# A hypergraph block on one core: H B Hᵀ made in two halves around v and y, and a last group finished graph by graph

## The reference, cut to what matters

```python
def hypergraph_conv(x, adj, W, b):
    H = (adj != 0).astype(x.dtype)
    w = adj.reshape(N, -1)[:, :C]                 # first row of adj
    Dn = 1 / einsum('nce,ne->nc', H, w)           # 0 where the sum is not positive
    Be = 1 / H.sum(axis=1)
    xw = einsum('ncd,hd->nch', x, W)
    m = Be[:, :, None] * einsum('nce,nch->neh', H, xw)
    return Dn[:, :, None] * einsum('nce,neh->nch', H, m) + b

h = layer_norm(relu(hypergraph_conv(x, adj, W1, b1)), gamma, beta)
y = hypergraph_conv(h, adj, W2, b2) + x
out = layernorm(x + y)                            # over the last axis, no gain
```

## Time and profile before

| | |
|---|---|
| median of 3 runs | 287.64 us (287.48 to 287.89) |
| the profiled execution, its own time | 287.23 us |
| its span in the trace | 285.4 us |
| PE busy | 276.9 us (97%) |
| PEld busy | 247.8 us (87%) |
| DVE busy | 229.5 us (80%) |
| ACT busy | 196.2 us (69%) |
| POOL busy | 134.9 us (47%) |
| granted TensorE clock, mean | 0.995 |

### The profile page before, as it was taken

The page is one execution under the profiler, slowest core; times in us unless marked ns, Lnnn a source line. Parts: engine busy times, 40 slices in busy tenths (PEclk is TensorE's granted clock), DMA queues, the critical chain, the costliest instruction groups (busy, mean ns, idle before and its releaser), DMA issues.

```text
span 285.4 us, 5786 instructions
## 1 busy us (share of the span) xinstructions
PE 276.9 (97%) x1820; PEld 247.8 (87%) x1820; DVE 229.5 (80%) x646; ACT 196.2 (69%) x560; POOL 134.9 (47%) x194
## 2 busy tenths in 40 slices
PE   7999999999999999999999999999999999999991
PEld 6889899898988989898998989899898989889890
DVE  3795688887889878887978878797987879696784
ACT  3588967877767678766767776676678775573714
POOL 2341546436372744536363553636364364526362
PEclk9999999999999999999999999999999999999998
DMA  6912042344324134433433333522423332020014
GB/s 217 332 52 69 3 129 39 92 126 116 114 63 158 57 97 128 111 113 92 147 54 119 112 92 112 111 94 55 149 39 92 94 93 76 37 73 3 21 54 147
DMA packets 37270, 27.70 MB, mean 97 GB/s; under 512 B 10028, under 2 KB 35320, under 8 KB 37240
## 3 DMA queue, kind: packets, MB, share of 16 engines
q1 hardware_dynamic: 37136, 27.30, 33.8%
q10 hardware_dynamic: 104, 0.04, 0.1%
HBM read 17.21 MB, written 8.42 MB: 90 GB/s over the span
## 4 chain that ended last, share of the span: by engine, by line
PE 91%; ACT 3%; DVE 3%; issue 1%; POOL 1%; DVEq 0%; POOLq 0%; ACTq 0%
PE bank_v L303 30%; PE bank_g L320 10%; PE bank_v L337 10%; PE bank_g L313 10%; PE bank_g L315 10%; PE bank_v L281 8%; PE bank_s L262 4%; PE bank_g L330 3%; PE bank_s L402 1%; ACT ht_sb L497 1%; ACT sq_sb L555 1%; PE bank_g L383 1%; DVE bn_sb L933 1%; DVE q_sb L742 0%; DVE pair_sb L735 0%
## 5 line engine op out<-in xcount | busy, mean ns | idle before, releaser
L981 POOL TENSOR_TENSOR xb_sb<-x_sb,b_half 128x512 f32<-128x512 f32 (+1 forms) x31 | 41.1, 1329 | 76.0 <-DVE r_lo L730 51.1
L548 ACT ACTIVATE r_sb<-bank_v,vec 128x512 f32<-128x512 f32 x64 | 44.2, 690 | 38.0 <-PE bank_v L303 37.4
L313 PE MATMUL bank_g<-w_hi,r_hi 128*128 128x258 f32 x256 | 65.6, 288 | 0.0
L315 PE MATMUL bank_g<-w_lo,r_hi 128*128 128x256 f32 x256 | 63.8, 282 | 0.0
L989 POOL TENSOR_SCALAR r_hi<-r_sb 128x512 fp32r<-128x512 f32 x64 | 43.6, 682 | 39.8 <-ACT r_sb L548 39.8
L303 PE MATMUL bank_v<-u_hi,w_lo 128*128 128x512 f32 x128 | 50.8, 397 | 0.0
L303 PE MATMUL bank_v<-u_lo,w_hi 128*128 128x512 f32 x128 | 50.8, 397 | 0.0
L303 PE MATMUL bank_v<-u_hi,w_hi 128*128 128x512 f32 x128 | 50.7, 396 | 0.0
L313 PEld LDWEIGHTS bank_g<-w_hi,r_hi 128*128 128x128 f32 x256 | 48.3, 189 | 1.7 <-DVE w_lo L798 0.3
L730 DVE TENSOR_TENSOR r_lo<-r_sb,r_hi 128x512 fp32r<-128x512 f32 x64 | 48.9, 785 | 0.9 <-POOL r_hi L989 0.9
L315 PEld LDWEIGHTS bank_g<-w_lo,r_hi 128*128 128x128 f32 x256 | 48.1, 188 | 1.2
(11 more groups left out here) (119 smaller groups left out, 457.6 us busy)
## 6 DMA issues: line engine op xcount, KB each, us to landing
x_sb<-in_x_dram SPq DMA_DIRECT2D x16, 512.0 KB, 3.9
out_dram<-z_sb SPq DMA_DIRECT2D x15, 512.0 KB, 3.2
adj_sb<-in_adj_dram SPq DMA_DIRECT2D x15, 256.0 KB, 3.7
d_row<-d_rows SPq DMA_DIRECT2D x13, 256.0 KB, 3.7
w_raw<-in_L_gnn_W_dram SPq DMA_DIRECT2D x2, 512.0 KB, 4.9
out_dram<-z_sb SPq DMA_DIRECT2D x2, 256.0 KB, 2.4
adj_sb<-in_adj_dram SPq DMA_DIRECT2D x2, 128.0 KB, 2.4
turned_h<-h_sb SPq DMA_TRANSPOSE x13, 2.4
```

What stands on the lines that cost most here:

```text
L313: pe.matmul(bank_g[:, n, 0:W2COLS], r_hi[:, i % 2, k, graph(n)], w2_hi[:, k], start=(k == 0), stop=False)
L315: pe.matmul(bank_g[:, n, 0:DOUT], r_hi[:, i % 2, k, graph(n)], w2_lo[:, k], start=False, stop=False, skip_group_check=True)
L548: nc.scalar.activation(r_sb[:, k], bank_v[:, k % 2], ACT.Relu, bias=vec[:, k:k + 1]).then_inc(relu_ready, 1)
L981: nc.gpsimd.tensor_tensor(xb_sb[:, i % 2, part], x_sb[:, i % 3, part], b2_half[:, :].unsqueeze(1).to_broadcast([P, n, DOUT]), ALU.add).the ...
```

## The change

- `make_s` takes a half. For iterations 1 to 12 half 0 of s(i+3) (graphs 0 and 1) is issued between v(i+1, 3) and y(i, 0), and half 1 stays behind y(i, 1).
- At the end DVE takes the statistics of group 14 for both halves before the last group's var1, and `make_var2` of group 14 before the last `read_g`.
- The last group's graphs 2 and 3 get their own steps: `make_last_var1(n)`, one POOL power of one column each, `read_last_g(n)`, one semaphore increment for each y matmul. PE issues the identity matmuls of graphs 2 and 3 behind y of graphs 0 and 1.
- Of the last group, graphs 0 and 1 are normalised by ACT and stored by SP as before; graph 2 is normalised by ACT, with a shift that POOL makes, and stored by a DMA from ACT's queue; graph 3 is normalised by DVE and stored by SP.
- Group 14 is stored as two halves of 256 KB instead of one of 512 KB.

```diff
@@ store (SP) @@
-                if i >= 1:
+                if 1 <= i < LAST:
+                    sp.wait_ge(out_ready, i)
                     store(i - 1)
-            for half in range(2):
-                store(LAST, half)
+            sp.wait_ge(half_out_ready, 1)
+            store(LAST - 1, graphs(0))
+            sp.wait_ge(out_ready, LAST)
+            store(LAST - 1, graphs(1))
+            sp.wait_ge(last_out_ready[0], 1)
+            store(LAST, graphs(0))
+            sp.wait_ge(last_out_ready[2], 1)
+            store(LAST, slice(3, 4))
@@ PE @@
-            def make_s(j):
-                pe.wait_ge(htb_ready, j + 1)
-                pe.wait_ge(wcol_ready, j + 1)
-                if j:
+            def make_s(j, half=None):
+                if half != 1:
+                    pe.wait_ge(htb_ready, j + 1)
+                    pe.wait_ge(wcol_ready, j + 1)
                     pe.wait_ge(a_ready, min(j, ON_PE))
                     pe.wait_ge(at_ready, j)
-                for n in range(PER):
+                for n in each(half):
                     mm = pe.matmul(s_parts[:, n // 2, n % 2], ht_sb[:, j % 2, n], htb_sb[:, j % 2, n],
                                    start=True, stop=True)
-                mm.then_inc(s_made, 1)
+                if half != 0:
+                    mm.then_inc(s_made, 1)
...
+                if i and i + 3 < G:
+                    make_s(i + 3, 0)
                 make_y(i, 0)
                 make_y(i, 1)
                 if i + 3 < G:
-                    make_s(i + 3)
+                    make_s(i + 3, 1 if i else None)
@@ PE, last group @@
+                for n in each(half):
+                    if n < 2:
+                        pe.wait_ge(z_ready, LAST * 2 - 1 + n)
+                    elif n == 2:
+                        pe.wait_ge(at_ready, G)
+                    else:
+                        pe.wait_ge(q_summed, G * 2)
+                    pe.matmul(last_z[n], ident_2[:, :], xb_sb[:, 1, n], start=True, stop=False)
+                for n in each(half):
+                    if half:
+                        pe.wait_ge(last_g_ready, n - 1)
+                    else:
+                        pe.wait_ge(g_ready, LAST * 2 + 1)
                     mm = pe.matmul(last_z[n], at_sb[:, LAST % 3, n], g_sb[:, n], start=False, stop=True)
@@ ACT, last group @@
+                for part, graphs_done in enumerate((each(0), [2])):
+                    act.wait_ge(last_shift2_ready, part + 1)
+                    for n in graphs_done:
+                        ins = nc.scalar.activation(z_sb[:, 1, n], last_z[n], ACT.Identity,
+                                                   bias=last_shift2[:, n:n + 1], scale=rstd2[:, 1, n:n + 1])
+                    ins.then_inc(last_out_ready[part], 1)
+                act.wait_ge(last_out_ready[1], 1)
+                act.dma_start(out_dram[:, LAST * PER + 2:LAST * PER + 3], z_sb[:, 1, 2:3]).then_inc(stored[1], 16)
@@ DVE, last group @@
+            def make_last_var1(n):
+                dve.wait_ge(last_g_made if n == 2 else g_made, 1 if n == 2 else G * 2)
...
+            def read_last_g(n):
+                dve.wait_ge(last_rstd1, n - 1)
...
+            take_stats2(LAST - 1, 0)
+            take_stats2(LAST - 1, 1)
             make_var1(LAST, 0)
-            take_stats2(LAST - 1, 1)
+            make_var2(LAST - 1)
+            make_last_var1(2)
             read_g(LAST, 0)
-            make_var1(LAST, 1)
-            make_var2(LAST - 1)
-            read_g(LAST, 1)
-            take_last_stats2(0)
-            make_var2(LAST, 0)
-            take_last_stats2(1)
-            make_var2(LAST, 1)
+            make_last_var1(3)
+            read_last_g(2)
+            read_last_g(3)
+            for half in range(2):
+                take_last_stats2(half)
+                make_var2(LAST, half)
@@ POOL, last group @@
-            for half in range(2):
-                inverse_std1(LAST, half)
+            inverse_std1(LAST, 0)
             inverse_std2(LAST - 1)
+            for n in each(1):
+                pool.wait_ge(last_var1, n - 1)
+                nc.gpsimd.tensor_tensor(rstd1[:, n:n + 1], stat1[:, 1, n:n + 1], half_power[:, n:n + 1],
+                                        ALU.pow).then_inc(last_rstd1, 1)
```

More of the change, by code:

```diff
@@ L101, in hypergraph_block @@
         shift2 = sb("shift2", [P, PER])
-        last_shift2 = sb("last_shift2", [P, PER // 2])
+        last_shift2 = sb("last_shift2", [P, PER])
         bank_s = ctx.enter_context(nc.psum_tensor("bank_s", [P, 2, BANK], F32))
@@ L148, in hypergraph_block @@
         var2_ready, rstd2_ready, shift2_ready = sem("var2_ready"), sem("rstd2_ready"), sem("shift2_ready")
-        out_ready, last_out_ready = sem("out_ready"), [sem("last_out_low"), sem("last_out_high")]
+        out_ready, last_out_ready = sem("out_ready"), [sem("last_out_low"), sem("last_out_2"), sem("last_out_3")]
         last_shift2_ready = sem("last_shift2_ready")
+        half_out_ready, last_g_made, last_step = sem("half_out_ready"), sem("last_g_made"), sem("last_step")
+        last_var1, last_rstd1, last_g_ready, last_y_made = (sem(f"last_{n}") for n in ("var1", "rstd1", "g_ready", "y_made"))
         def graph(n):
@@ L200, in load_d, with store @@
                     [P, P * PER])).then_inc(d_row_in[j % 2], 16)
[L202 to L208, removed]
+            def store(i, part=slice(0, PER)):
+                sp.dma_start(out_dram[:, i * PER + part.start:i * PER + part.stop],
                              z_sb[:, i % 2, part]).then_inc(stored[i % 2], 16)
@@ L323, in make_g @@
                     mm.then_inc(g_made, 1)
+                elif i == LAST and n == 2:
+                    mm.then_inc(last_g_made, 1)
             def turn_q(i):
@@ L470, in _ @@
             pe.wait_ge(xb_ready, G * 2)
[L471 to L478, removed]
             for half in range(2):
-                pe.wait_ge(g_ready, LAST * 2 + half + 1)
                 for n in each(half):
+                    if n < 2:
[10 more added lines that the diff above has]
+                        pe.wait_ge(g_ready, LAST * 2 + 1)
                     mm = pe.matmul(last_z[n], at_sb[:, LAST % 3, n], g_sb[:, n], start=False, stop=True)
-                mm.then_inc(y_made, 1)
+                    if half:
+                        mm.then_inc(last_y_made, 1)
+                if half == 0:
+                    mm.then_inc(y_made, 1)
         @block.scalar
@@ L563, in normalise @@
                     ins.then_inc(out_ready, 1)
+                elif i == LAST - 1:
+                    ins.then_inc(half_out_ready, 1)
             def sum_q(i):
@@ L575, in normalise_last @@
             def normalise_last():
-                act.wait_ge(last_shift2_ready, 1)
                 act.wait_ge(stored[1], landed(LAST - 2, 2))
[L579 to L582, removed]
+                for part, graphs_done in enumerate((each(0), [2])):
[6 more added lines that the diff above has]
+                act.dma_start(out_dram[:, LAST * PER + 2:LAST * PER + 3], z_sb[:, 1, 2:3]).then_inc(stored[1], 16)
             act.dma_start(edge_rows[:, :], adj[:, 0, :]).then_inc(edges_in, 16)
@@ L925, in _ @@
                     make_z(i, 1)
-            take_stats2(LAST - 1, 0)
+            def make_last_var1(n):
+                dve.wait_ge(last_g_made if n == 2 else g_made, 1 if n == 2 else G * 2)
+                dve.wait_ge(q_summed, G * 2)
+                nc.vector.scalar_tensor_tensor(out=stat1[:, 0, n:n + 1], in0=bank_g[:, n, MEAN:MEAN + 1],
+                                               scalar=bank_g[:, n, MEAN + 1:MEAN + 2], in1=sum_sq[:, n:n + 1],
+                                               op0=ALU.mult, op1=ALU.add).then_inc(last_step, 1)
+                dve.wait_ge(last_step, n - 1)
+                nc.vector.tensor_scalar(stat1[:, 1, n:n + 1], stat1[:, 0, n:n + 1], 0.0, EPS, ALU.max,
+                                        ALU.add).then_inc(last_var1, 1)
@@ L928, in take_last_stats2 @@
+            def read_last_g(n):
+                dve.wait_ge(last_rstd1, n - 1)
+                nc.vector.scalar_tensor_tensor(out=g_sb[:, n], in0=bank_g[:, n, 0:DOUT], scalar=rstd1[:, n:n + 1],
+                                               in1=c2[:, :], op0=ALU.mult, op1=ALU.add).then_inc(last_g_ready, 1)
             def take_last_stats2(half):
-                dve.wait_ge(y_made, LAST * 2 + (half + 1))
                 if half == 0:
+                    dve.wait_ge(y_made, LAST * 2 + 1)
                     dve.wait_ge(mean2_ready, LAST)
@@ L932, in take_last_stats2 @@
                 for n in each(half):
+                    if half:
+                        dve.wait_ge(last_y_made, n - 1)
                     ins = nc.vector.bn_stats(bn_sb[:, n], last_z[n])
                 ins.then_inc(stats_ready, 1)
+            take_stats2(LAST - 1, 0)
+            take_stats2(LAST - 1, 1)
             make_var1(LAST, 0)
-            take_stats2(LAST - 1, 1)
+            make_var2(LAST - 1)
```

(21 more changed lines are left out.)

4 lines of the change are left out of this document (2 added, 2 removed).

## The result

The changed kernel takes 285.47 us (median of 4 runs, 285.31 to 285.77) against 287.63 us, a ratio of 0.9931 with a 95% interval of 0.9918 to 0.9943: 2.2 us faster. Its profiled execution took 285.38 us, with a span of 283.6 us instead of 285.4.

What follows compares the result with a forecast made beforehand. PE, busy 97% of the span, was taken to bound the main loop, but no longer the end. Loop 1.8 us plus end 0.74 us, summed as 2.6 us, gave a median of 285.0 us, range 283.8 to 286.4.

Steps and rivals of the forecast that it cites:

- y's wait on relu: Main loop, y half 1: half of s put before y removes the wait for relu, giving PE 0.24 us an iteration.
- What is late next: Main loop: y and q end 0.20 us later, turn_q waits 0.14 us for q, leaving 0.15 us an iteration.
- 12 x 0.15 = 1.8 us: Main loop: gain of 0.15 us in each of iterations 1 to 12; bounds 0.4 and 2.9 us in all.
- z half 0: Main loop on DVE: starts at 219.80 at the latest, ends near 220.47, before u's first load at 220.82; does not bind.
- All four rivals: q does not bind, 0.17; q eats nearly all the loop's gain, 0.11; slower, 0.04; the end gives nothing, 0.06.
- (d): Rival: the end gives nothing, with single-column powers at 0.71 us and ACT's queue at 2.5 us; 285.8 us; chance 0.06.
- The order at the end: Last group: group 14's statistics before var1 and single-column powers of 0.54 us start bn_stats 0.31 us earlier.
- The last z: Last group: graph 3 on DVE, graph 2 on ACT; last z at 282.10 instead of 282.64, 0.54 us earlier.
- The stores: End: the last store, 128 KB from ACT's queue with nothing queued ahead, lands in 2.1 us, at 284.23.
- The whole end: New order, split z and stores together end the span 0.74 us earlier; bounds nearly 0.0 and 1.2 us.
- The 0.54 that followed from the Trainium skill's figure: End, alternative size: 2.0 us fixed plus bytes at 436 GB/s, 2.3 us for 128 KB; gain 0.54 instead of 0.74 us.
- Signs of it: Changed profile: turn_q waits for q in some 14 iterations, 0.1 to 0.2 us each; iterations 16.26 us apart.

Runs made afterwards that it cites:

- loop_only: The kernel before with only the split of s (half 0 between v and y in iterations 1 to 12) and the old ending: 285.63 us, ratio 0.9952.
- whole_s_first: The changed kernel with all of s(i+3) ahead of y in iterations 1 to 12: 290.44 us, ratio 1.0118 to the kernel before.
- q_inside_g: The changed kernel with turn_q issued between the r_hi and r_lo matmuls of g's first graph: 283.58 us, ratio 0.9875 to the kernel before.
- q_inside_g_old_s: The changed kernel with turn_q moved inside g's first graph and s whole again behind y: ratio 0.9957 to the kernel before.
- one_power: The changed kernel with the last group's graphs 2 and 3 sharing one power, graph 2's variance moved behind read_g(LAST, 0): ratio 0.9957 to the kernel before.
- g14_whole: The changed kernel with group 14 stored in one transfer of 512 KB: ratio 0.9927 to the kernel before.
- split_z_one_store: The changed kernel with the last group's graphs 2 and 3 still normalised by ACT and DVE, but stored by SP in one 256 KB transfer: ratio 0.9922 to the kernel before.

## Why the prediction was right

It forecast 285.0 us with a range of 283.8 to 286.4; the result is 285.47. The gain is 2.2 us where 2.6 was forecast. (Its two terms, 1.8 and 0.74, make 2.54, so by its own sum the forecast was 285.1 us.)

- **y's wait on relu.** Right in mechanism and size: 0.24 us an iteration forecast, 0.23 gone from the chain, and loop_only shows it by itself.
- **What is late next.** Right: q was forecast 0.14 us late, to leave 0.15 us an iteration. In ten of the twelve iterations turn_q's loads come 16.27 us apart instead of 16.41. whole_s_first and the pair q_inside_g and q_inside_g_old_s show that this is the chain y, z, q and not a price of splitting s: push y further and the iteration grows, take q out of the way and the 0.10 us come back, but only with the split.
- **12 x 0.15 = 1.8 us** was 0.2 too much: the loop gave 1.57 us. Ten iterations gave 0.146 each, 1.46 us. Iteration 1 gave 0.10 and iteration 2 lost 0.05; the 0.06 that are left came in iterations 13 and 14, which have no s. Iteration 2 and the next one, in the kernel after:

```profile
72.73 1.28 DVE L777 SCALAR_TENSOR_TENSOR z_sb<-xb_sb,bank_v 128x512 f32<-128x512 f32 x2 [0.64 <-PE bank_v L345]
73.54 1.86 PEld L287 LDWEIGHTS bank_v<-at_sb,x_sb 128*128 128x128 f32 x16 [0.19 <-issue]
...
88.85 1.44 DVE L777 SCALAR_TENSOR_TENSOR z_sb<-xb_sb,bank_v 128x512 f32<-128x512 f32 x2 [0.28 <-PE bank_v L345]
89.74 1.86 PEld L287 LDWEIGHTS bank_v<-at_sb,x_sb 128*128 128x128 f32 x16
```

In iteration 2 DVE idles 0.36 us longer ahead of z half 0, with no releaser that explains it; in the kernel before it came late there too (72.11 us, behind 0.19 us put down to issue). With y later, that delay reaches u, which idles for 0.19 us. The prediction let z half 0 start 1.0 us ahead of u "at the latest"; it starts 0.9 us ahead, so u had less slack than it summed. I summed one iteration twelve times, and held z and q to repeat to a few hundredths, without looking for the one that differs; why DVE is late there stays open. All four rivals fell, (d) by powers of 0.55 us and a landing of 2.2.
- **The order at the end.** Right: bn_stats 0.31 us earlier forecast, 0.28 measured. Single-column powers took 0.55 us each, forecast 0.54. Of the 0.60 us that one_power loses, about 0.26 come from sharing the power and the rest from where graph 2's variance stands.
- **The last z.** Right in time: 0.54 us earlier forecast, 0.53 measured. But the prediction let the span end a fixed time after it, and the stores' data show another limit: before, 1.05 MB in one unbroken stretch, of which group 14's 512 KB came first. By these rows an earlier last z alone would have gained nothing there; it mattered because the change also took group 14 out of the way. No run makes one without the other.
- **The stores.** This term was mis-sized: 0.20 us for a smaller store in an emptied queue. From the last z's end to the span's end it took 2.73 us (280.87 to 283.6) instead of 2.76 (282.64 to 285.4). The landing was 2.2 us, not 2.1, and g14_whole and split_z_one_store show that neither the halves nor ACT's queue do anything. The prediction took the last store as one "with nothing queued ahead"; the 256 KB of graphs 0 and 1 run right ahead of it. The whole end gave 0.56 us where 0.74 was forecast, and that it came so near is partly luck: it is 1.5 us less of data against a first issue 0.96 us later, and neither is a term of the sum. The 0.54 that followed from the Trainium skill's figure ("DMA: Bandwidth & Descriptors", "Anatomy of one DMA — SWDGE (gpsimd) path") was nearer by luck too. The page gives that formula for transfers that GpSimd issues, and these come from SP and ACT; by it 256 KB would take an estimated 2.6 us, where such a store with nothing ahead of it took 2.1 to 2.2.
- **Signs of it.** I had said that a wait of turn_q for q would show some 14 times. The list of waits still has it twice, and the twelve short ones are not in it; they were found only by setting q's end beside turn_q's start.

## What to carry to other kernels

When a wait on the bound engine is filled with work from behind it, everything that hangs on the delayed instruction moves by what was put in less what was saved (0.445 - 0.24 us here); follow that chain to the place where it comes back to the bound engine, and compare with the slack there (turn_q had 0.35 us to q; q came 0.20 us later and PE would have come 0.24 us earlier, 0.44 together). If it does not fit, look for work to put at that second place as well. Here moving four transposes behind eight matmuls gave another 1.5 us, some 0.4 of it in iteration 13: the best kernel of this study takes 283.6 us, 1.25% less than the kernel before.

At an end where stores run behind each other, look at the DMA engines first: if their data have no gap, the end follows from when the first of those stores is issued and from the bytes behind it, and neither splitting transfers nor a second queue helps. What made room here was that the earlier group's store left before. The other half of it is the slow small instruction that the first store waits for: begin it on the first piece that is ready.

## What the runs showed of the hardware

- A store with nothing queued ahead landed 2.1 to 2.2 us after its issue for 256 KB, and 2.9 to 3.0 for the 512 KB of group 14. Behind another store, 256 KB took 2.3 and 2.5 us in the kernel before, and 128 KB 2.0 to 2.2 in the others. No run has 128 KB alone. Data started 0.85 us after the issue and moved at some 340 GB/s.
- POOL's power takes 0.55 us for one column, 0.70 to 0.71 for two and 1.02 for four.
- The startup ends at any of several moments, 42.31 to 43.02 us at q of group 1, for the same instructions. In the execution shown above it was W1's load that landed late. A median over few runs can carry 0.3 us of that; a distance inside the trace does not.
